# Feed-forward stage of a two-layer block: scaled product kept in its PSUM bank, maxima over pairs, eight chunks of tap tiles, silu and second product two chunks behind

## What is computed

```python
def act_quant(x):
    scale = 127.0 / clip(max(abs(x), axis=-1), 1e-05)
    return clip(round(x * scale), -128, 127) / scale
def weight_quant(w):
    scale = 1.0 / clip(mean(abs(w)), 1e-05)
    return clip(round(w * scale), -1, 1) / scale
h = einsum('bsd,hd->bsh', act_quant(layernorm(x)), weight_quant(w1))   # 512 -> 2048
h = conv over s, per channel, three taps, zero padding, + conv_b
h = silu(h)
x = x + einsum('bsd,hd->bsh', act_quant(h), weight_quant(w2))          # 2048 -> 512
```

## Time and profile before

| | us |
|---|---|
| median of 3 runs | 3205.28 (3201.35 to 3208.55) |
| profiled execution | 3201.77 |
| its span, first to last instruction | 3200.0 |
| PE, DVE, ACT, POOL busy | 2567.4, 1706.6, 1198.8, 982.6 |
| mean granted TensorE clock | 0.911 |

### The profile page before, as it was taken

How to read it: one execution, slowest core, us unless ns; L and a number is a source line. 1 busy time by engine, 2 the same in 40 slices (tenths; PEclk the granted TensorE clock), 3 DMA queues, 4 the chain that set the end, 5 groups by cost and what they waited for, 6 DMA issues and landing times. The chain is left out here.

```text
span 3200.0 us, 46927 instructions
## 1 busy us (share of the span) xinstructions
PE 2567.4 (80%) x15834; PEld 1339.4 (42%) x15835; DVE 1706.6 (53%) x2416; ACT 1198.8 (37%) x1810; POOL 982.6 (31%) x804
## 2 busy tenths in 40 slices
PE   8799983566656588888888049999999999999970
PEld 5566651222222344444443024444444444444430
DVE  4455548899897766666655622233333333333225
ACT  2344433778876455555554311111111111111110
POOL 0233321667767111111110630032235503340017
PEclk9899995888988799999989579999999999999995
DMA  5360001000000200000003520022123302220028
GB/s 212 111 228 11 1 1 53 1 1 1 0 1 0 61 13 9 8 8 8 8 5 93 198 107 31 28 72 72 53 85 112 111 28 74 78 89 26 33 61 277
DMA packets 90378, 189.40 MB, mean 59 GB/s; under 512 B 25738, under 2 KB 28810, under 8 KB 89770
## 3 DMA queue, kind: packets, MB, share of 16 engines
q1 hardware_dynamic: 64922, 97.91, 9.4%
q0 software_dynamic: 25360, 90.21, 8.6%
HBM read 120.13 MB, written 67.96 MB: 59 GB/s over the span
## 5 line engine op out<-in xcount | busy, mean ns | idle before, releaser
L2080 PE MATMUL e_gate_up<-weights,e_x_t 128*128 x3456 | 771.2, 380 | 1.4 <-ACT e_x_t L2134 1.4
L2080 PEld LDWEIGHTS e_gate_up<-weights,e_x_t 128*128 128x128 bf16 x3456 | 332.6, 98 | 376.6 <-issue 3.9
L2167 DVE TENSOR_TENSOR e_mid<-e_gate,e_gate_up 128x512 f32<-128x512 f32 x144 | 98.9, 687 | 645.1 <-ACT e_gate L2140 645.1
L2100 PE MATMUL e_out<-weights,e_mid_t 128*128 x1728 | 384.7, 379 | 1.1 <-DVE e_mid_t L2180 1.1
L2140 ACT ACTIVATE e_gate<-e_gate_up 128x512 f32<-128x512 f32 x144 | 86.0, 597 | 683.6 <-PE e_gate_up L2080 683.6
L2100 PEld LDWEIGHTS e_out<-weights,e_mid_t 128*128 128x128 bf16 x1728 | 169.1, 98 | 204.8 <-issue 1.2
L766 POOL TENSOR_TENSOR a_probs<-a_e,a_probs 128x616 bf16<-128x616 f32 x64 | 85.6, 1353 | 517.5 <-ACT a_probs L1000 517.5
L1359 PE MATMUL f_out<-f_w,hidden 128*128 128x512 f16 x512 | 141.2, 402 | 101.5 <-ACT hidden L1461 100.8
L1289 POOL TENSOR_TENSOR f_shared<-f_shared 128x512 f32<-128x512 f32 x128 | 181.0, 1415 | 122.2 <-DVE f_shared L1567 122.2
L1278 POOL TENSOR_TENSOR hidden<-hidden,f_up_row 128x512 f32<-128x512 f32 x128 | 178.5, 1405 | 86.6 <-ACT f_up_row L1490 86.6
L2030 POOL TENSOR_TENSOR e_token<-e_token 1x1 f32<-1x1 f32 x6 | 1.1, 183 | 657.7 <-PE e_out L2100 657.7
(11 more groups left out here) (254 smaller groups left out, 4458.6 us busy)
## 6 DMA issues: line engine op xcount, KB each, us to landing
raw_weights<-in_w POOLq DMA_DIRECT2D x72, 512.0 KB, 4.0
sorted_x<-a_zero_row POOLq DMA_DIRECT2D x1, 18432.0 KB, 55.6
e_x_rows<-sorted_x SPq DMA_DIRECT2D x72, 256.0 KB, 2.7
sorted_y<-e_y_rows SPq DMA_DIRECT2D x72, 256.0 KB, 2.0
raw_weights<-in_w SPq DMA_DIRECT2D x24, 512.0 KB, 4.1
x<-in_x SPq DMA_DIRECT2D x4, 2048.0 KB, 21.1
out<-x SPq DMA_DIRECT2D x32, 256.0 KB
hidden<-in_w_t SPq DMA_DIRECT2D x1, 4096.0 KB, 17.1
```

Source lines behind the costliest of these rows:

```text
L2080: last = nc.tensor.matmul(gate_up[half][:, part, :], x_t[:, u, a, k, :], plan.weights13[:, bass.ds(expert % 2, 1), b, k, col:col + 512], s ...
L2100: last = nc.tensor.matmul(out[:, :], mid_t[:, a, j, :], plan.weights2[:, bass.ds(expert % 2, 1), b, j, :], start=(j == 0 and a == b == 0), ...
L2167: nc.vector.tensor_tensor(mid[:, half, :], gate[:, half, :], gate_up[half][:, 1, :], ALU.mult).then_inc(mid_made, 1)
```

## The change

Six things. (1) `scale_down` writes its result back into the product's PSUM bank, and the taps and the third tap read it there; the padded tile is gone, and shifted taps cover 511 columns. (2) There are three product banks instead of two; chunk j uses bank j % 3, but chunk 15 bank 1, and `first` waits for the third tap of the chunk that held the bank (1's is 15 of the batch before, 15's is 13, two chunks back; else three or four). The front's transposes move into scales_bank to make room, so the first flip waits for copy_row, and the tail's transposes for the front's copies. (3) Eight y and side tiles for four. (4) ACT's step j becomes silu(j-2), round_up(j), taps(j+2), then the front; taps(b+1, 1) thus stands ahead of the tail. (5) DVE's step j does the third tap of j first and scale_down(j+2) behind it. (6) Maxima over eight pairs, six of them in the loop, behind steps 4, 6, ... 14. PE's second product runs two chunks behind (LAG = 2) and flip goes from steps 8 and 11 to 9 and 12.

```diff
@@ -1169,8 +1169,8 @@
 
     HID = 4 * D
     HC = HID // P
-    BUF = 4
-    GROUPS = ((0, 5), (5, 10), (10, 14), (14, HC))
+    BUF = 8
+    GROUPS = tuple((lo, lo + 2) for lo in range(0, HC, 2))
     FULL = 127.0
     SMALLEST = 1e-5
     def low_halves(a):
@@ -1185,10 +1185,10 @@
         w1 = sb("w1", [P, KD, HID], BF16)
         w2 = sb("w2", [P, HC, D], F16)
         shared = sb("shared", [P, HC * D])
-        quarter = HC * D // 4
+        half = HC * D // 2
         hq = low_halves(hidden[:, :, :])
-        y = shared[:, 2 * quarter:3 * quarter].rearrange("p (c n) -> p c n", c=BUF)
-        side = shared[:, 3 * quarter:].rearrange("p (c n) -> p c n", c=BUF)
+        y = shared[:, 0:half].rearrange("p (c n) -> p c n", c=BUF)
+        side = shared[:, half:].rearrange("p (c n) -> p c n", c=BUF)
         raw = (hidden[:, :, :].rearrange("p c n -> p (c n)"), shared[:, :])
         sums = sb("sums", [P, 2])
         mean = sb("mean", [P, 2])
@@ -1209,18 +1209,22 @@
         xq = low_halves(xn[:, :, :])
         xq_t = sb("xq_t", [P, 2, KD, S], BF16)
         down_row = sb("down_row", [P, 2, S])
-        padded = sb("padded", [P, BUF, S + 2])
         tops = sb("tops", [P, 2, S])
         top2 = sb("top2", [P, TPS])
         up2 = sb("up2", [P, TPS])
         down2 = sb("down2", [P, TPS])
         up2_row = sb("up2_row", [P, S])
 
-        product = [pb(f"product{i}", [P, 512]) for i in range(2)]
+        product = [pb(f"product{i}", [P, 512]) for i in range(3)]
         out = [pb(f"out{i}", [P, 512]) for i in range(TPS)]
-        front = pb("front", [P, 2, 512], F16)
-
         scales_bank = pb("scales_bank", [P, 512])
+
+        front = scales_bank[:, :].bitcast(F16).rearrange("p (i n) -> p i n", i=2)
+
+
+        bank_of = [*(j % 3 for j in range(HC - 1)), 1]
+        turns = bank_of * 2
+        since = [next(d for d in range(1, HC) if turns[HC + j - d] == turns[HC + j]) for j in range(HC)]
 
         w2_in = sem("w2_in"); small_in = sem("small_in"); zeroed = sem("zeroed")
         sums_made = sem("sums_made"); sums_ready = sem("sums_ready"); weights_made = sem("weights_made")
@@ -1269,8 +1273,6 @@
             nc.gpsimd.tensor_copy(ident_16[:, :], core.ident[:, :]).then_inc(zeroed, 1)
             nc.gpsimd.memset(ones_16[:, :], 1.0).then_inc(zeroed, 1)
             nc.gpsimd.memset(minus[:, :], -OFFSET / P).then_inc(zeroed, 1)
-            nc.gpsimd.memset(padded[:, :, 0:1], 0.0).then_inc(zeroed, 1)
-            nc.gpsimd.memset(padded[:, :, S + 1:S + 2], 0.0).then_inc(zeroed, 1)
 
             def iteration(b, parity, has_middle, has_back, has_front):
                 def scale_up(j):
@@ -1286,8 +1288,8 @@
                     scale_up(j + 2)
                     if has_middle:
                         pool.wait_ge(left_added, HC * b + j + 1)
-                        nc.gpsimd.tensor_tensor(y[:, j % BUF, :], y[:, j % BUF, :], side[:, j % BUF, :], ALU.add
-                                                ).then_inc(right_added, 1)
+                        nc.gpsimd.tensor_tensor(y[:, j % BUF, 0:S - 1], y[:, j % BUF, 0:S - 1],
+                                                side[:, j % BUF, 0:S - 1], ALU.add).then_inc(right_added, 1)
 
             iterations(pool, iteration)
 
@@ -1301,6 +1303,8 @@
             def flip(n, pair):
 
                 pe.wait_ge(rounding, TPS * n + 2 * pair + 2)
+                if pair == 0:
+                    pe.wait_ge(row_copied, n + 1)
                 at_least(pe, front_copied, TPS // 2 * n + pair)
                 for i in range(2):
                     for k in range(KD):
@@ -1323,19 +1327,18 @@
             scales_row(0)
             for pair in range(TPS // 2):
                 flip(0, pair)
-            pe.wait_ge(row_copied, 1)
+            pe.wait_ge(front_copied, TPS // 2)
             weight_sums(1)
             pe.wait_ge(weights_made, 2)
             for j in range(HC):
                 last = nc.tensor.matmul(out[0][:, :], ones_16[:, :], w2[:, j, :], start=(j == 0), stop=(j == HC - 1))
             last.then_inc(columns_ready, 1)
-            pe.wait_ge(front_copied, TPS // 2)
 
             def first(b, j, parity):
 
-                at_least(pe, scaled_down, HC * b + j - 1)
+                at_least(pe, left_added, HC * b + j - since[j % HC] + 1)
                 for k in range(KD):
-                    last = nc.tensor.matmul(product[j % 2][:, :], w1[:, k, j % HC * P:(j % HC + 1) * P],
+                    last = nc.tensor.matmul(product[bank_of[j % HC]][:, :], w1[:, k, j % HC * P:(j % HC + 1) * P],
                                             xq_t[:, parity, k, :], start=(k == 0), stop=(k == KD - 1))
                 last.then_inc(product_ready, 1)
 
@@ -1360,7 +1363,7 @@
                                                 start=False, stop=(j == HC - 1))
                     last.then_inc(hq_used, 1)
 
-                LAG = 1
+                LAG = 2
                 for j in range(HC + LAG):
                     if has_middle and j + 2 < HC:
                         first(b, j + 2, parity)
@@ -1370,13 +1373,13 @@
                         first(b, j + 2, 1 - parity)
                     if has_front and j == 7:
                         scales_row(b + 1)
-                    if has_front and j in (8, 11):
-                        flip(b + 1, j // 11)
+                    if has_front and j in (9, 12):
+                        flip(b + 1, j // 12)
                     second(j - LAG)
 
                 if has_middle:
                     pe.wait_ge(tops_made, b + 1)
-                    at_least(pe, row_copied, b + 1 + has_front)
+                    pe.wait_ge(front_copied, TPS // 2 * (b + 1 + has_front))
                     for i in range(TPS):
                         last = nc.tensor.transpose(scales_bank[:, i * P:(i + 1) * P], tops[:, 0, i * P:(i + 1) * P],
                                                    core.ident[:, :])
@@ -1439,12 +1442,14 @@
 
                 act.wait_ge(scaled_down, HC * b + j + 1)
                 at_least(act, hidden_made, HC * b + j + 1 - BUF)
-                nc.scalar.activation(y[:, j % BUF, :], padded[:, j % BUF, 1:S + 1], ACT.Identity,
+                scaled = product[bank_of[j % HC]]
+                nc.scalar.activation(y[:, j % BUF, :], scaled[:, :], ACT.Identity,
                                      bias=column(conv_b, j % HC), scale=conv_w[:, j % HC, 1:2])
-                nc.scalar.activation(side[:, j % BUF, :], padded[:, j % BUF, 2:S + 2], ACT.Copy,
+                nc.scalar.activation(side[:, j % BUF, 0:S - 1], scaled[:, 1:S], ACT.Copy,
                                      scale=conv_w[:, j % HC, 2:3]).then_inc(taps_made, 1)
 
             taps(0, 0)
+            taps(0, 1)
 
             def iteration(b, parity, has_middle, has_back, has_front):
                 done = b - 1
@@ -1466,11 +1471,11 @@
                         round_up(j)
                 if has_middle:
                     for j in range(HC):
-                        if j + 1 < HC or has_front:
-                            taps(b, j + 1)
+                        if j > 1:
+                            silu(j - 2)
                         round_up(j)
-                        if j > 0:
-                            silu(j - 1)
+                        if j + 2 < HC or has_front:
+                            taps(b, j + 2)
                         if has_front:
                             if j in (0, 1):
                                 normed(b + 1, 2 * j)
@@ -1482,6 +1487,7 @@
                                 copy_row(b + 1, 1 - parity)
                             elif j in (9, 12):
                                 copy_front(b + 1, j // 12, 1 - parity)
+                    silu(HC - 2)
                     silu(HC - 1)
 
                 if has_middle:
@@ -1526,14 +1532,13 @@
             ternary(0, w1_in, w1)
             scales(0)
             ternary(1, w2_in, w2)
-            dve.wait_ge(zeroed, 8)
+            dve.wait_ge(small_in, 32)
 
             def scale_down(b, j, parity):
                 dve.wait_ge(product_ready, HC * b + j + 1)
-                at_least(dve, taps_made, HC * b + j + 1 - BUF)
-                at_least(dve, left_added, HC * b + j + 1 - BUF)
-                nc.vector.tensor_tensor(padded[:, j % BUF, 1:S + 1], product[j % 2][:, :], down_row[:, parity, :],
-                                        ALU.mult).then_inc(scaled_down, 1)
+                bank = product[bank_of[j % HC]]
+                nc.vector.tensor_tensor(bank[:, :], bank[:, :], down_row[:, parity, :], ALU.mult
+                                        ).then_inc(scaled_down, 1)
 
             dve.wait_ge(row_copied, 1)
             scale_down(0, 0, 0)
@@ -1556,17 +1561,17 @@
                         result(nc.vector.tensor_tensor(tops[:, 0, :], tops[:, 0, :], tops[:, 1, :], ALU.max))
 
                 for j in range(HC):
+                    if has_middle:
+                        dve.wait_ge(taps_made, HC * b + j + 1)
```

(8 more changed lines are left out.)

## The result

The changed kernel takes 3217.08 us (median of 6, 3214.92 to 3218.91) against 3206.88 for the kernel before: ratio 1.0037, interval 1.0025 to 1.0049. It is slower, by 10 us between the medians. The profiled execution took 3217.26 us, and its span is 3215.5 us against 3200.0, 15.5 longer; the kernel before was profiled near the low end of its runs (3201.35 to 3208.55).

A forecast was written before the change was run, and what follows sets the result against it. DVE was taken as fullest (55.55 of 61 us), ACT next. Middle batches at 65.15 against 61.45 gave +22 for six; -2.4 (first of six), -2.4 (first batch) and -6.4 (last full) left +11: 3201.8 becomes 3213, range 3187 to 3228.

The forecast's parts named there:

- slower: Whole program: more than 6.4 us above the profiled 3201.8; chance 0.43.
- (c): Step 9: ACT's silu(7) waits for its second product, queued on PE behind the flip that waits for copy_row; 2.9 us.
- (a): Batch start: ACT waits 1.5 us for GpSimd's first product, then 2.4 for DVE's scaling of chunk 2; together 3.9.
- (d): Step 13: chunk 15's first product waits for chunk 13's third tap, second(11) queues behind, silu(11) waits; 0.7 us.
- (e): Step 15: next batch's first product waits for chunk 15's third tap, so silu(13) waits; taken at 3.0 us.
- (f): Batch tail: last silu to last maximum 2.0 us instead of 4.3, then 5.34 to the next f_up_row copy; 7.35.
- (b): Steps 1 to 8: go at ACT's pace, DVE's pair of steps 5.0 us against ACT's 4.74 plus its extras.
- the rival with dearer PSUM: DVE's scaling in place: costs its upper bound, 4.5 us on DVE; about +2.7 a batch, total 3230; chance 0.12.
- the warm case: Hand-overs at steps 9 and 15: PE stays at 2.4 GHz, waits 1.9 and 2.0 us; total 3199; chance 0.24.
- The faster case: Loop: a pair of maxima takes 2.0 us and the clock holds; a batch 60.9, total 3186; chance 0.20.
- The one in which the third tap still meets GpSimd: DVE's third tap: still blocked by GpSimd, at the same price as dearer PSUM writes; no separate chance given.
- That blocking: DVE and GpSimd block each other where DVE's inputs both lie in SBUF; third tap 1201 ns against 740.

The follow-up runs named there:

- the first edit: Changed kernel with PE's flip placed behind the second product instead of ahead of it: 3198.44 us, ratio 0.9981 against the kernel before.
- the norms: Changed kernel with ACT's four normed instructions all in step 0: 3218.84 us, ratio 1.0051 against the kernel before.
- the SBUF edit: Changed kernel whose third tap reads the side tile in SBUF instead of the product's bank, leaving out the left tap: 3243.53 us, ratio 1.0123.
- all three: Changed kernel with the second product ahead of first product and flip in every step, and the four normed in step 0: 3196.28 us, ratio 0.9973.

## Why the prediction was right, and where its steps were off

The forecast was 3213 us, range 3187 to 3228, slower the likeliest of the three at 0.43; measured were 3217.08. The mechanism, (c), was named, and the first edit shows it. A middle batch was put at 65.15 us; the six take 64.8 on average. The 3213 was nearer than the steps behind it: the forecast +11 stands against 10.2 between the medians, but 15.5 between the profiled executions. Term by term, for the batch from 725.16, which takes 65.03:

| term | forecast | measured | row |
|---|---|---|---|
| ACT's own work | 47.3 | 47.65 | 65.03 less the waits |
| (a) start | 3.9 | 3.48 | 1.38 at 727.13, 2.10 at 729.96 |
| (c) step 9, flip | 2.9 | 2.92 | 758.93 |
| (d) step 13 | 0.7 | 2.20 | 773.04 |
| (e) step 15 | 3.0 | 1.35 | 779.25 |
| (f) tail | 7.35 | 7.43 | 790.19 |

The agreement of the sum is better than that of its terms.

- **(d) and (e)** missed by 1.5 and 1.65 us with opposite signs. That is one batch: in the six, (c) is 2.91 to 3.08, (d) 0.28 to 2.35 and (e) 1.34 to 2.99, and (d) and (e) together are 3.0 to 3.8 in each, where 3.7 was forecast. What ACT loses in (d) it does not lose again in (e), where it arrives later; their sum was right, their parts were not. In this batch the third tap of chunk 13 came late behind DVE's own waits and a combining maximum (3.39 at 759.79, 1.23 at 764.98, the maximum of 1.34 at 767.51), PE stood 4.15 us, and the eight matmuls took 3.3 us (769.70 to 772.95) where 1.9 would do at full clock.
- **DVE at step 9** was not priced. Queued behind the flip stands not only a second product but, behind that, the next first product, for which DVE waits 3.39 us. With the flip moved behind, DVE's longest wait for a product is 2.2.
- **(b) and (a).** Steps 1 to 8 did go at ACT's pace: it waits for nothing between 729.96 and 758.93. But it had little room: when the norms filled its wait at the start, it waited for GpSimd instead. The first of the six batches shows the same. The wait at its taps(2) is absent, as forecast, but 1.33 comes at 611.36 and 0.35 at 614.47, and the batch takes 64.78, where the forecast's -2.4 puts it at 62.75. The account of ACT's time was right as a description, wrong as a list of what could be won.
- **DVE's work** was to fall by 8 to 9 us. Over exactly a batch (717.07 to 778.64, and 725.16 to 790.19) it falls from 56.1 to 49.0, by 7.2. The third taps bring the 7.3 and the reductions the 4.3 that were counted; the combining maxima take 4.7 more (6.9 for 2.2) instead of 2.9, since this sum left out their blocking.
- **The third tap** was put at 740 ns and takes 746. **Scaling in place** takes 694 ns, and 0.59 from start to start (755.06 to 755.65), where 0.62 was taken between 0.60 and 0.90; the rival with dearer PSUM is out. The Trainium skill, VectorE: DVE Perf Modes, The TRN2 errata, gives a PSUM source 62 cycles more than one in SBUF, 1.0 us a batch by the estimate made above; the third tap's 746 ns from PSUM against the 740 of an unblocked one from SBUF show no such cost here.
- **ACT's taps from PSUM** were to be 0.04 less each. The tap with one pointer (L1448) takes 686 ns, the one with two (L1446) 775; before they took 711 and 806 (L1444 and L1442), so the two bring 0.9 us a batch instead of 1.3. Own work of 47.65 against 47.3 leaves that term about right.
- **Maxima.** A combining maximum takes 0.69 alone, 0.99 on average and 1.73 at worst (747.49); the bound of 1.15 was too low, since it came from the third tap's mean loss and not from the longest one.
- **First batch:** -2.4 was forecast, +1.0 measured. It was walked as bound by DVE's work. The banks are now held until the third tap, and from 535 to 595 DVE waits seven times for a product, 13.5 us, against twice, 6.5, before; 6.8 and 6.1 of these are one wait each. That wait was left out.
- **Last full batch:** -6.4 forecast, -3.2 measured; 51 to 52 us was to be its length, 54.7 it is. It was said to have no (c) and (e), so to go at GpSimd's pace. ACT's silu waits for f_out at 995.09, 1010.65, 1025.32 and 1031.25, 7.0 us in all, 2.58 of it behind the second product of chunk 0 and 2.69 behind a first product that waited 3.46 for its bank.

Together the two end batches were 6.6 us too cheap and the middle ones right in sum (+20.2 for +19.8, the first 2.0 too cheap and the other five 0.3 each too dear), which is the distance from the forecast +11 to the measured +18; 2.5 us came back outside the stage. That they did, and that 3213 fits so well, is luck. The sums of the rivals contain a slip: the warm case takes -3.6 and the faster one -4 for the first batch, for which the forecast has -2.4, and no reason is given; it moves neither by more than 2 us. On the rivals: the warm case needed PE at 2.4 GHz in (c), and the granted clock there is 0.50. The faster case would have needed (d) and (e) near zero. The one in which the third tap still meets GpSimd falls with the SBUF edit.

That blocking: the Trainium skill, SBUF — State Buffer, Who interferes with whom, says that a VectorE instruction with two SBUF inputs contends with a GpSimd instruction that reads SBUF, and that one with at most one SBUF input, outside the two-port modes, does not. The rows agree: 1229 and 1201 ns against 746, and the maxima of pairs (one input) stay at 1225 to 1233 ns beside the same GpSimd work.

Open is what the fall of the clock costs by itself: no run kept PE busy through the waits and changed nothing else. An estimate from the rows: the flip and the second product behind it take 2.72 us at 0.50 (756.12 to 758.84) and 1.75 in the kernel before (741.80 to 743.55), so some 1.0 of the 2.92 of (c) is the clock. A fourth product bank, which might break the ring of "all three", was not tried: the stage already holds eight banks, three for product, four for out and the shared one. Nor was another bank than that of chunk 13 for chunk 15.

## What to carry to other kernels

On an engine that works in order, price a moved instruction by everything queued behind it, and follow each of those to who waits for it: here a transpose that waited for a copy held up a second product (ACT) and a first product (DVE). Keep the instruction that must wait last in its step, and put work for the next round where an engine waits anyway, as the taps in the tail. A list of an engine's waits tells where the time is, not what the removal of each brings: three different edits to PE's order gave 17 to 19 us each, and two of them together with the norms 21.

## What had not been expected

- Four groups instead of eight pairs: the same regrouping of the maxima was worth 4 us in one order and 37 in the other. The long reductions cost little where DVE was the busiest engine and PE waited 0.2 us for a bank, and much where a bank with a first and a second product queued for it was freed behind them.
- The reductions themselves do not grow with the number of elements alone: two chunks take 1.23 us, four 3.67 (766.91 in the kernel before), five 4.62 (756.16), so 0.61 us a chunk in pairs and 0.92 in the longer groups. A reduction of 2048 elements that lie next to each other (L1518, 549.01) takes 2.28 for the 3.67 of four chunks. No run shows why.
- A combining maximum of two SBUF tiles beside GpSimd took 1.73, 1.09 and 1.34 us at three places of one batch, for 0.69 alone; in the kernel before with pairs 1.29 on average.
- DVE read and wrote the same PSUM bank at 694 ns (L1540), against 685 from PSUM to SBUF in the kernel before with pairs: writing back in place costs 9 ns.
